# Reordering the slots of three attention stages of a decoder on one NeuronCore: transposes ahead of scores, split projections, narrower waits

## What is computed

```
x = x + L0_attn (layernorm(x))               # self: 16 heads of 64, rotary, causal, biases
x = x + L0_xattn(layernorm(x), ctx, ctx)     # cross0: 16 heads of 32, causal, no biases
x = x + L0_ffn  (layernorm(x))               # 32 experts, each takes its top tokens
x = x + L1_attn (layernorm(x))               # q * sum(k*v), normalised q and k
x = x + L1_xattn(layernorm(x), ctx, ctx)     # cross1: 16 heads of 32, all pairs, biases
x = x + L1_ffn  (layernorm(x))               # fp8-rounded linear
```

```
q = x W_Q + b_Q; k = y W_K + b_K; v = y W_V + b_V    # y = x in self, ctx in cross
p = softmax(q k' / sqrt(d))                          # causal in self and cross0
out = concat_h(p v) W_O + b_O
```

## Time and profile before

| what | value |
|---|---|
| time, median of 3 runs | 4296.71 us (4296.22 to 4300.49) |
| profiled execution: its own time | 4302.26 us |
| its span, first to last instruction | 4300.4 us |
| mean granted clock of PE | 0.909 |
| self, cross0, cross1 in the span | about 80 to 1400, 1450 to 2140, 3400 to 4130 us |
| busy over the span | PE 3525.5, PEld 2423.8, DVE 1963.1, POOL 1427.6, ACT 1258.2 us |
| mean of one copy out of T by DVE, self (L767) | 548 ns |
| mean of one addition by POOL for a turned tile (L382, L384) | 1277 to 1288 ns |

### The profile page before, as it was taken

The page is one execution under the profiler, slowest core; times in us unless marked ns, Lnnn a source line. Parts: engine busy times, 40 slices in busy tenths (PEclk is TensorE's granted clock), DMA queues, the critical chain, the costliest instruction groups (busy, mean ns, idle before and its releaser), DMA issues. The chain is left out here.

```text
span 4300.4 us, 70717 instructions
## 1 busy us (share of the span) xinstructions
PE 3525.5 (82%) x23116; PEld 2423.8 (56%) x23116; DVE 1963.1 (46%) x4934; ACT 1258.2 (29%) x4320; POOL 1427.6 (33%) x2092
## 2 busy tenths in 40 slices
PE   4999999998998799999857666655999699999955
PEld 3665666666665577777626111112777577777732
DVE  5444444444443455555450000001566456656657
ACT  2222222222222345445410000001111355555521
POOL 2444444445343233333310000000222145454437
PEclk9999999999998799999985877877999799999976
DMA  5000000000000211111166999996111211111114
GB/s 117 16 20 15 24 15 20 24 15 20 24 15 10 80 49 49 47 50 44 35 218 249 427 429 426 428 426 256 62 67 59 78 50 39 49 49 39 49 52 132
DMA packets 158786, 459.15 MB, mean 107 GB/s; under 512 B 47392, under 2 KB 51872, under 8 KB 138208
## 3 DMA queue, kind: packets, MB, share of 16 engines
q1 hardware_dynamic: 150272, 445.72, 27.3%
q10 hardware_dynamic: 8448, 12.59, 0.8%
HBM read 402.17 MB, written 56.10 MB: 107 GB/s over the span
## 5 line engine op out<-in xcount | busy, mean ns | idle before, releaser
L404 POOL TENSOR_TENSOR cross_prob<-cross_prob,cross_rsum 128x256 f32<-128x256 f32 (+1 forms) x1024 | 564.7, 573 | 767.6 <-DVE cross_rsum L761 767.5
L617 ACT ACTIVATE cross_prob<-cross_S,cross_neg_max 128x256 f32<-128x256 f32 (+1 forms) x1024 | 445.2, 457 | 55.1 <-DVE cross_neg_max L754 30.3
L617 ACT ACTIVATE self_prob<-self_S,self_neg_max 128x128 f32<-128x128 f32 (+1 forms) x512 | 210.4, 419 | 569.2 <-DVE self_neg_max L754 569.2
L404 POOL TENSOR_TENSOR self_prob<-self_prob,self_rsum 128x128 f32<-128x128 f32 (+1 forms) x512 | 248.4, 508 | 383.8 <-DVE self_rsum L761 383.3
L528 PE MATMUL cross_T<-cross_ident,cross_prob 128*128 128x128 f32 x1792 | 289.2, 278 | 83.2 <-ACT cross_probT L625 75.8
L528 PEld LDWEIGHTS cross_T<-cross_ident,cross_prob 128*128 128x128 f32 x1792 | 205.2, 142 | 144.7 <-issue 83.7
L1171 PE MATMUL experts_H<-moe_w,experts_tok 128*32 128x512 f32 x1024 | 169.4, 822 | 134.1 <-DMA moe_b<-in_L_ffn_w 129.6
L625 ACT ACTIVATE cross_probT<-cross_T 128x384 f32<-128x384 f32 (+1 forms) x256 | 139.8, 546 | 421.8 <-PE cross_T L528 421.7
L472 PE MATMUL self_A<-self_wo_f,self_zT 128*128 128x512 f32 x512 | 253.7, 654 | 0.6 <-DVE self_zT L776 0.6
L617 ACT ACTIVATION_READ_ACCUMULATOR cross_prob<-cross_S,cross_neg_max 128x1 f32 x1024 | 221.8, 217 | 0.0
L1189 PE MATMUL experts_O<-moe_w,experts_hidT 128*32 128x512 f32 x1024 | 172.8, 837 | 52.3 <-DMA moe_w<-in_L_ffn_w 44.8
(11 more groups left out here) (270 smaller groups left out, 8900.8 us busy)
## 6 DMA issues: line engine op xcount, KB each, us to landing
moe_w<-in_L_ffn_w SPq DMA_DIRECT2D x64, 4096.0 KB, 34.4
cross_x_t<-x SPq DMA_DIRECT2D x32, 512.0 KB, 4.0
cross_c_t<-in_ctx SPq DMA_DIRECT2D x32, 512.0 KB, 4.9
cross_res<-x SPq DMA_DIRECT2D x32, 512.0 KB, 3.5
x<-cross_res SPq DMA_DIRECT2D x32, 512.0 KB, 2.8
self_x_t<-in_x SPq DMA_DIRECT2D x16, 512.0 KB, 3.6
self_res<-in_x SPq DMA_DIRECT2D x16, 512.0 KB, 3.5
x<-self_res SPq DMA_DIRECT2D x16, 512.0 KB, 2.8
```

The costliest lines, as they stand in the source:

```text
L404: ins = pool.tensor_tensor(pr, pr, rsum[:, i, t:t + 1].to_broadcast([P, KQ[t]]), ALU.mult)
L617: ins = act.activation(prob[:, h % NP, SOFF[t]:SOFF[t] + KQ[t]], SC[h % 4][:, SOFF[t]:SOFF[t] + KQ[t]], ACT.Exp, bias=neg_max[:, h, t:t + ...
```

## The change

- `PLAN`, self: ("V", 1, 0) goes from slot 5 to 2 and ("V", 1, 1) from slot 6 to 5.
- `PLAN`, cross: ("Q", 3) is cut in halves by a new list `EARLY`, its first half (the queries) in slot 2, its second (the keys) in slot 3. ("O", 0) is cut too, in slots 7 and 9. ("O", 1) goes from 9 to 10, the X transposes from 10 to 11, the context's from 11 to 13, query uses 0 and 1 of the next batch from 13 and 14 to 14 and 15. The statistics go from slot 5 to 6, the normalisation from 7 to 8.
- PE does `prob_transposes` first in each slot, then `times_v` and `scores`.
- ACT does `probs_odd`, `exps`, `heads_hi`; DVE does `probs_even`, `maxima`, `sums_inverse`, `heads_done`.
- The wide waits become waits for the last X use, in self ahead of ("+", "P", 0, 0, 0) alone. In cross the keys' half of ("+", "Q", 0) waits for the last context use.

```diff
-def split_products(pe, out, pairs):
-
+def split_products(pe, out, pairs, part=None):
+
+    half = len(pairs) // 2
     for i, ((ah, al), (bh, bl)) in enumerate(pairs):
+        if part is not None and part != i // half:
+            continue
...
-        PLAN[5] += [("V", 1, 0)]
-        PLAN[6] += [("V", 1, 1)]
+        PLAN[2] += [("V", 1, 0)]
+        PLAN[5] += [("V", 1, 1)]
...
         PLAN[1] += [("Q", 2)]
-        PLAN[2] += [("Q", 3)]
+        EARLY[2] += [("Q", 3)]
+        PLAN[3] += [("Q", 3)]
         PLAN[5] += [("V", 0, 0)]
         PLAN[6] += [("V", 0, 1)]
-        PLAN[8] += [("O", 0)]
-        PLAN[9] += [("O", 1)]
-        PLAN[10] += [("+", "X", 0), ("+", "X", 1)]
-        PLAN[11] += [("+", "C", 0), ("+", "C", 1)]
-        PLAN[13] += [("+", "Q", 0)]
-        PLAN[14] += [("+", "Q", 1)]
+        EARLY[7] += [("O", 0)]
+        PLAN[9] += [("O", 0)]
+        PLAN[10] += [("O", 1)]
+        PLAN[11] += [("+", "X", 0), ("+", "X", 1)]
+        PLAN[13] += [("+", "C", 0), ("+", "C", 1)]
+        PLAN[14] += [("+", "Q", 0)]
+        PLAN[15] += [("+", "Q", 1)]
...
-        STATS_AT, APPLY_AT = 5, 7
+        STATS_AT, APPLY_AT = 6, 8
...
             def body(b, first, last):
                 for i in range(H):
+                    if not (first and i < T_LAG):
+                        prob_transposes(b, i - T_LAG)
                     if i % G == 0:
                         if not (first and i < V_LAG):
                             times_v(b, i - V_LAG, first, last)
                         scores(b, i, first, last)
-                    if not (first and i < T_LAG):
-                        prob_transposes(b, i - T_LAG)
-                    for key in PLAN[i]:
+                    for key, part in [(k, 1 if k in SPLIT else None) for k in PLAN[i]] + [(k, 0) for k in EARLY[i]]:
...
-                        if key in (("+", "P", 0, 0, 0), ("+", "Q", 0)):
-                            pe.wait_ge(a_free, u)
+                        ctx_use = None
+                        if key == (("+", "P", 0, 0, 0) if rotary else ("+", "Q", 0)):
+                            pe.wait_ge(a_free, uses.at(("+", "X", 1), b, first, last) + 1)
+                            if key[1] == "Q":
+                                ctx_use = uses.at(("+", "C", 1), b, first, last)
...
@@ ACT body @@
-                    if not (first and i < Z_LAG):
-                        heads_hi(b, i - Z_LAG, first, last)
                     if not (first and i < T_LAG):
                         probs_odd(b, i - T_LAG)
                     for j in EXP_AT[i % G]:
                         exps(b, i - i % G + j)
+                    if not (first and i < Z_LAG):
+                        heads_hi(b, i - Z_LAG, first, last)
...
@@ DVE body @@
+                    if not (first and i < T_LAG):
+                        probs_even(b, i - T_LAG)
+                    for j in MAX_AT[i % G]:
+                        maxima(b, i - i % G + j)
+                    if not (first and i < 1):
+                        sums_inverse(b, i - 1)
                     if not (first and i < Z_LAG):
                         heads_done(b, i - Z_LAG, first, last)
-                    for j in MAX_AT[i % G]:
-                        maxima(b, i - i % G + j)
-                    if not (first and i < T_LAG):
-                        probs_even(b, i - T_LAG)
-                    if not (first and i < 1):
-                        sums_inverse(b, i - 1)
```

More of the change, by code:

```diff
@@ L159, in attention_phase @@
     PLAN = [[] for _ in range(H)]
+    EARLY = [[] for _ in range(H)]
     if rotary:
@@ L180, in attention_phase @@
         PLAN[1] += [("Q", 2)]
-        PLAN[2] += [("Q", 3)]
+        EARLY[2] += [("Q", 3)]
+        PLAN[3] += [("Q", 3)]
         PLAN[5] += [("V", 0, 0)]
         PLAN[6] += [("V", 0, 1)]
-        PLAN[8] += [("O", 0)]
-        PLAN[9] += [("O", 1)]
-        PLAN[10] += [("+", "X", 0), ("+", "X", 1)]
-        PLAN[11] += [("+", "C", 0), ("+", "C", 1)]
-        PLAN[13] += [("+", "Q", 0)]
-        PLAN[14] += [("+", "Q", 1)]
+        EARLY[7] += [("O", 0)]
[5 more added lines that the diff above has]
+        PLAN[15] += [("+", "Q", 1)]
         BEFORE = [("X", 0), ("X", 1), ("C", 0), ("C", 1), ("Q", 0), ("Q", 1)]
-        STATS_AT, APPLY_AT = 5, 7
+        STATS_AT, APPLY_AT = 6, 8
         LATE_V = {0: ("V", 0, 1)}
+    SPLIT = [key for step in EARLY for key in step]
     N_W = 0 if rotary else 4 * KD
@@ L419, in bank_for, with proj_tokens, extra @@
                 after(pe, a_free, u - 1)
-            def proj_tokens(u, bank, src, w, t, c):
-                bank_for(u)
-                split_products(pe, A[bank][:, :], [
+            def proj_tokens(u, bank, src, w, t, c, part):
+                if part != 1:
+                    bank_for(u)
+                mm = split_products(pe, A[bank][:, :], [
                     ((src[0][:, k, t * P:(t + 1) * P], src[1][:, k, t * P:(t + 1) * P]),
                      (w[0][:, k, c * 512:(c + 1) * 512], w[1][:, k, c * 512:(c + 1) * 512])) for k in range(KD)
-                ]).then_inc(a_full, 1)
-            def extra(key, u, bank, n):
+                ], part)
+                if part != 0:
+                    mm.then_inc(a_full, 1)
+            def extra(key, u, bank, n, part=None, ctx_use=None):
                 kind = key[0]
@@ L444, in extra @@
                 elif kind == "P":
-                    proj_tokens(u, bank, xT, (wqs, wks)[key[1]], key[3], key[2])
+                    proj_tokens(u, bank, xT, (wqs, wks)[key[1]], key[3], key[2], part)
                 elif kind == "V":
-                    proj_tokens(u, bank, xT if rotary else cT, wvs, key[2], key[1])
+                    proj_tokens(u, bank, xT if rotary else cT, wvs, key[2], key[1], part)
                 elif kind == "Q" and rotary:
@@ L459, in extra @@
                     g = key[1]
-                    bank_for(u)
+                    if part != 1:
+                        bank_for(u)
                     for j, (w, src) in enumerate(((wqs, xT), (wks, cT))):
+                        if part is not None and part != j:
+                            continue
+                        if j == 1 and ctx_use is not None:
+                            pe.wait_ge(a_free, ctx_use + 1)
                         mm = split_products(pe, A[bank][:, j * S:(j + 1) * S], [
@@ L464, in extra @@
                              (src[0][:, k, :], src[1][:, k, :])) for k in range(KD)])
-                    mm.then_inc(a_full, 1)
+                    if part != 0:
+                        mm.then_inc(a_full, 1)
                 elif kind == "O":
                     t = key[1]
-                    pe.wait_ge(z_ok, n * NT + NT)
-                    bank_for(u)
+                    if part != 1:
+                        pe.wait_ge(z_ok, n * NT + NT)
+                        bank_for(u)
                     if rotary:
@@ L474, in extra @@
                     else:
-                        split_products(pe, A[bank][:, :], [
+                        mm = split_products(pe, A[bank][:, :], [
                             ((zTs[0][:, k, t * P:(t + 1) * P], zTs[1][:, k, t * P:(t + 1) * P]),
-                             (wos[0][:, k, :], wos[1][:, k, :])) for k in range(KD)]).then_inc(a_full, 1)
+                             (wos[0][:, k, :], wos[1][:, k, :])) for k in range(KD)], part)
+                        if part != 0:
+                            mm.then_inc(a_full, 1)
             if not rotary:
@@ L561, in body @@
                             continue
-                        u = uses.at(key, b, first, last)
-                        if key in (("+", "P", 0, 0, 0), ("+", "Q", 0)):
-                            pe.wait_ge(a_free, u)
-                        extra(key[ahead:], u, uses.bank(key, b, first, last), b + 1 if ahead else b - 1 if key[0] == "O" else b)
+                        ctx_use = None
[3 more added lines that the diff above has]
+                                ctx_use = uses.at(("+", "C", 1), b, first, last)
+                        extra(key[ahead:], uses.at(key, b, first, last), uses.bank(key, b, first, last),
+                              b + 1 if ahead else b - 1 if key[0] == "O" else b, part, ctx_use)
             def tail(b):
                 for i in range(V_LAG):
+                    if i < T_LAG:
+                        prob_transposes(b, i - T_LAG)
                     if i % G == 0:
                         times_v(b, i - V_LAG, False, False)
-                    if i < T_LAG:
-                        prob_transposes(b, i - T_LAG)
                 for t in range(T):
```

8 lines of the change are left out of this document (4 added, 4 removed).

## The result

The changed kernel takes 4454.0 us (median of 4 runs, 4449.71 to 4457.28) against 4296.47 us: the ratio is 1.0365, 95% interval 1.0349 to 1.0382. It is 157 us slower. The forecast was 122 us slower, 4419 us. The two profiled executions took 4302.26 and 4449.71 us, so what is read from the traces adds up to 147.5 us; the other 10 are the choice of executions.

What follows compares the result with a forecast made beforehand. PE was taken as the bound, 91 to 92% busy, losing time to waits and self's clock. Self +40, cross0 +30, cross1 +34 and cross clock +18 make 122; 4302.3 + 122 - 5.6 = 4419 us, range 4330 to 4495.

Steps and rivals of the forecast that it cites:

- Slots 7, 10 and 12: Self: transposes placed first wait for POOL's normalised probabilities, 1.95, 2.0 and 2.0 us a batch.
- The 1.4 us of slot 0: Self, slot 0: transposes wait 1.4 us for head 14 from POOL, mostly taking what narrowing the wait gave.
- Slot 3 then has none: Self, slot 3: no wait left, since the moved value projection fills 2.9 us in slot 2.
- 2.0 us of slow clock: Self: 2.0 us a batch lost to slow clock goes, and half of it, 1.0, returns with the new waits.
- 5.6 us of waits: Cross0, slots 8, 10, 11 to 12 and 13 to 14: new waits of 1.4, 1.0, 0.8 and 2.4 us a batch.
- scaling cross0 by the ratio of the waits of before: Cross1: waits scaled from cross0 by 4.1/3.7, giving 6.2 against 4.1 us a batch, +34 us.
- A: All attention stages: other engines run ahead, new waits are half; 85 us less, 4212 us; chance 0.13.
- B: Only self loses: the context's chain at slot 14 is half as long, cross ends even; 4337 us; chance 0.15.
- C: Clock: each wait of about 2 us is followed by 3.41 us at half clock; 128 us more, 4547; chance 0.14.
- the first: Sign in self: forecast wrong if PE's waits stay under 6 us a batch.
- The second: Sign in cross: forecast wrong if no wait over 1.5 us shows.
- The third: Sign on the clock: forecast wrong if clock 0.50 appears more than once a batch.

Runs made afterwards that it cites:

- The run with the narrow wait and V: Kernel before, self only: wait ahead of the next batch's first projection only for the last X use, slot 5's value projection moved to slot 2; 4219.07 us.
- the run further tuned: Self: kernel before, narrowed wait, V in slots 2 and 6, earlier z read and query use 0; cross: changed kernel with reordered ACT and DVE work; 4109.33 us.
- the two cross edits: Changed kernel with statistics and normalisation of x back in slots 5 and 7, and the context ahead of exponentials and maxima in slot 13; 4336.88 us.
- the run with the statistics: Changed kernel with the statistics and the normalisation of the next x back in slots 5 and 7; 4437.81 us, ratio 1.0325.

## Why the prediction was right, and where it was not

The direction and the mechanism held, the size was 35 us short. Part of that closeness is luck. By stage, with the expected clock in it, I had +40, +39 and +43 us and found +64, +23 and +61: two stages too low, one too high, 26 us in all; the other 9 are the choice of executions.

- **Self, waits.** Forecast 9.8 us a batch, found 10.3 against 6.3. Slots 7, 10 and 12 were 1.95, 2.0 and 2.0 and came out at 1.88, 2.00 and 1.99. Slot 2 came out at 2.0 for 2.45. The 1.4 us of slot 0 came as two: 0.69 there, and 0.71 in slot 15, where the projection waits for the bank of slot 14's. The step that failed is "Slot 3 then has none": the output projection waits 0.98 us there for the last z, whose read stands on DVE behind the copy of the value projection that moved to slot 2. The run with the narrow wait and V, in which DVE reads z first in a slot, has it too (0.87), so it is not the new place of the read. In the run further tuned, which reads z a slot earlier, it is gone.
- **Self, clock.** The failed term. I took off 2.0 us of slow clock and let half of it return. The trace has 1.5 stretches of 3.41 us a batch at 0.50, some 2.6 us lost, where before had 1.25, some 2.1. So none of it went, and a little came on top. With the waits' 4.0 us this gives, within 0.2 us, the 4.3 us by which a batch grew, and so self's +64, where I had 40.
- **Cross0.** Forecast 5.6 us of waits, found 5.2: 1.23 (1.4) in slot 8, 0.78 (1.0) in slot 10, where POOL's head 7 is the last and not DVE's copy, 0.77 (0.8) in slot 11, 0.89 + 1.50 (2.4) in slot 14. So 1.5 us a batch over the 3.7 of before, 24 us, and the stage is 23 us longer. The clock, for which I gave half of the 18 us, stood at 0.99 and took little.
- **Cross1.** Found 85.6 us in 12 batches, 7.1 us each, against 4.1; forecast 6.2. The step that failed is scaling cross0 by the ratio of the waits of before, instead of summing slot by slot. Slots 8 and 10 have 1.26 each, slot 14 1.31 and 1.46. And slot 3 has one that cross0 lacks, because POOL adds the bias of the output to res between the normalisation of head 15 and that of head 0:

```profile
3642.86 2.54 POOL L418 TENSOR_TENSOR cross_res<-cross_res,cross_bo_r 128x512 f32<-128x512 f32 x2
3645.37 2.31 POOL L412 TENSOR_TENSOR cross_prob<-cross_prob,cross_rsum 128x256 f32<-128x256 f32 x4
```

```profile
3646.59 0.66 PE L548 MATMUL cross_T<-cross_ident,cross_prob 128*128 128x128 f32 x4 [1.05 <-POOL cross_prob L412]
```

  3.0 us for 16 batches are 48 of the 61; the clock of 0.98 in place of 1.00, at most 1.0 us of a batch of 49, is the rest.
- **Splitting the projections** cost nothing by itself, as forecast: without the waits, a batch of cross0 has as much work as before within 0.1 us where the clock does not fall (44.70 - 5.2 = 39.5, against 43.29 - 3.7 = 39.6).
- **Rivals.** A (the new waits are half) is out: nearly every wait was within 0.5 us of its forecast. B (cross even) is out in the changed kernel; with the two cross edits, cross1 is as long as before and cross0 35 us shorter. C (the clock) was partly right: of the eight waits of about 2 us in two batches of self, three were followed by slow clock, and in the run with the statistics the clock took most of a real gain. The Trainium skill (TensorE: Matmul & The Clock Gate, HAM oscillation — how this bites in real kernels) tells of a kernel in which every pass of a loop starts cold again; the rows of that run show it here at waits of 0.90 and 1.50 us with 0.5 us of transposes between them, once a batch.
- **The signs.** Of the three that would have shown the forecast wrong, the first stayed out (self has 10.3 us of waits a batch). The second stands on its edge: it asked for a wait over 1.5 us in cross, and the longest of a batch are 1.50 in cross0 and 1.46 in cross1. The third came: clock 0.50 appears more than once a batch in self, three times in two. Of the others, POOL is waited for five times a batch in self, but one of the five is 0.69 us and not 2; and the turn, which I had gone from the projections, holds up that of slot 15.

What stays open: why the pair of waits in slot 14 dropped the clock in nearly each batch in that run and in far fewer of the changed kernel, where it is just as long. The batch is 44.4 us long in the one and 44.7 in the other; no run varied that length alone.

## What to carry to other kernels

An instruction that may have to wait belongs behind the work that is ready, so compare the time at which its data are done with the start of the slot, not with its old place. When work is moved to cover a wait, list what it brings along and what it leaves bare: its copy came to stand ahead of the read of z, and the slot that it left no longer covered the next such read. With one wait that came back at a bank, this took a third of the gain that I had expected. The order of PE is the largest flaw of the change: without it, self gains 43 us where it lost 64. The stages need not share one order. The fastest kernel has Z and S first in self and the transposes first in cross, with the steps that the cross slots wait for moved ahead on their own engines, and is 4.4% faster than before. No run has those cross edits with Z and S first, so what the order by itself is worth in cross is not shown.

## What the runs showed that I had not expected

Two edits of the cross stages gave 16 and 55 us alone and 117 together. The first took 1.6 us of waits from a batch of cross0, and PE then spent 3.41 us of nearly each batch at a granted clock of 0.50, which costs up to 1.7 us. The batch shrank from 44.70 to 44.37 us, so only 0.3 of the 1.6 us was left. A gain in waits can be lost for the most part to the clock, so both columns of the window have to be read for each variant.
